# The second attention's Q, K and V projections in three fp16 passes from its third batch on

## The chip, the cores and the metric

One NeuronCore of a Trainium2 chip runs the whole program. The metric is the device time of one execution, in microseconds, lower is better. TensorE is PE in the rows, VectorE is DVE, ScalarE is ACT, GpSimd is POOL, and SyncE (SP) only issues DMAs here.

## The reference

Four layers, each an attention and then a feed-forward, work on `x` of 8 batches x 256 tokens x 128 channels, each on a layer norm of `x` with its result added to `x`. Context `ctx_1024` has the same shape. The second attention is the one that changes:

```python
q = (query @ Wq.T + bq).reshape(B, S, H, dh).transpose(0, 2, 1, 3)      # H = 16, dh = 8
k = (key @ Wk.T + bk)...;  v = (value @ Wv.T + bv)...                    # key = value = ctx
scores = jnp.einsum('bhqd,bhkd->bhqk', q, k) / SCALE + chemical_bias[:, None, :, :]
scores = jnp.where(mask == 0, -jnp.inf, scores)
attn = jax.nn.softmax(scores, axis=-1)
out = jnp.einsum('bhqk,bhkd->bhqd', attn, v)...
return out @ Wo.T + bo
```

Around it stand, in order: a wide attention (head size 64), a feed-forward over 16 experts, this attention, a feed-forward of 8 routed experts and a shared one (layer 1), a retention with a gated feed-forward (layer 2), and an attention of the same kind without mask and bias (layer 3) with a last feed-forward.

## The kernel before

The kernel writes one program for each of the five engines. Order between engines comes from semaphores alone; on one engine the instructions stand in the order in which the code issues them. `narrow_attention(layer, ...)` builds both the second attention (`layer == 1`, `masked`) and the fourth (`layer == 3`).

It goes over 8 batches with 8 units each; a unit `u` is a pair of heads, `b, n = divmod(u, 8)`. On TensorE a unit is: `weigh(u)` (L735 the shifts, L739 the transposed scores), on odd `n` `maxima` (L725, transposes of the row maxima's parts), `scores(u + 3)` (L709, and L716 adds bias and mask), `mix` (L757, probabilities by values), then, on `n` 0 to 4, `project(b + 1, n)`, a job of the next batch's projections, and on `n == 5` `out(b - 1)` (L778, L782), the output product. Jobs 0 to 3 are Q and K for half of the heads each (L684), job 4 is V (L695). Masked, each job is two fp32 matmuls, which the profile shows as four records; in the fourth attention each is made of three fp16 passes (L688, L698): weights and inputs are held as a high and a low fp16 half, and the products high x high, high x low and low x high are summed (`PASSES`).

VectorE takes in each unit the bias and mask add of the transposed scores (L937), the row maximum (L920) of the unit three ahead, on odd ones of these `cut` (L927, L929: the maxima in parts, which L725 transposes), and around it the norm of the next sublayer: `stats` (L299, L302, L305) at `n == 7`, `scale` (L330) at `n == 1`, and `norm_out` (L957, L960) and the add to `x` (L965). ScalarE does the exponentials (L857), copies the projections out of PSUM with bias and scale (L836, L841), and copies the shifts (L851).

GpSimd runs one list in order for each batch `b`: `masks_beside(b, 0)` (L911, L913), four `split_` of the projections into halves (L632, L636), `masks_beside(b, 1)`, after batch 1 `lead.weights` (the halves of the next feed-forward's weights, L2056 to L2066), then `power` of the norm two batches back (L310) and `lead.halves` (L2076, L2078). Its turn for batch `b` runs while the other engines are on the units of batch `b - 1`. In the fourth attention `weights16` (L605 to L610) halves the attention's weights, scaled by 256 in place, and `inputs16` (L620, L622) a batch's context and `xn_t`. The context tile is double-buffered and loaded by SyncE (`loads`). The retention's two loads of the context (`LOADS = 2`, L2737) are waited for by `keys` on GpSimd (L2726 on), behind the memsets of `zeros` (L2743).

## Time and profile before

| what | us |
|---|---|
| median of three runs | 1470.1 |
| lowest, highest | 1463.5, 1475.24 |
| the profiled execution: time | 1461.97 |
| its span | 1460.2 |
| second attention, about | 738 to 994 of the span |

Over the whole span TensorE is busy 90%, VectorE 71%, GpSimd 63%, ScalarE 62%; the mean granted TensorE clock is 0.956 of the full 2.4 GHz. A row of windows gives a stretch and its length, then the busy us (and instructions) of PE, PEld (weight loads), DVE, ACT and POOL, the granted TensorE clock as a share of 2.4 GHz, the DMA share and GB/s. Rows give times in us from the span's start, or durations in ns where they say so. In a line `out<-in` comes the shape (partitions x elements, type) and xcount; in brackets stands the idle time of the engine just before it and what ended it. Starts of instructions on one engine may overlap a little, as they are pipelined.

### The profile page before, as it was taken

The numbers are of one execution on the slowest core, as the hardware profiler recorded it, in microseconds if no ns is written. First come the engines' busy times: TensorE is split into PE (matmuls) and PEld (weight loads), VectorE is DVE, ScalarE is ACT, GpSimd is POOL, SyncE is SP. The second block draws the span as 40 slices with busy tenths as digits, with TensorE's granted clock in tenths as the row PEclk, the third lists the DMA queues.
The fourth block names the chain that finished last, engine by engine and source line by source line (L and its number), as shares of the span: only waits on it lengthen the run. The fifth ranks groups of instructions, "written<-read, shape, count | busy, mean of one in ns | idle before, by whom it ended". The sixth has DMA issues, their size and how long they took to land.

```text
span 1460.2 us, 37325 instructions
## 1 busy us (share of the span) xinstructions
PE 1318.7 (90%) x14582; PEld 807.8 (55%) x14582; DVE 1039.4 (71%) x2493; ACT 899.9 (62%) x1487; POOL 913.2 (63%) x879
## 2 busy tenths in 40 slices
PE   5999999997979999999979999986989799799987
PEld 3466566665757777777743433433567466344435
DVE  7888888888744344444647989986698477677775
ACT  4677787774859999999934544432234332465556
POOL 6788887876658999899857646522262120655535
PEclk9899999999989999999968999997989899799999
DMA  8000000000013110000101021000000000000000
GB/s 276 9 9 9 9 9 9 2 2 17 29 34 100 60 34 29 29 29 14 67 4 33 34 66 33 31 2 29 1 2 3 8 1 1 8 9 5 5 2 30
DMA packets 26083, 39.64 MB, mean 27 GB/s; under 512 B 7314, under 2 KB 13365, under 8 KB 25429
## 3 DMA queue, kind: packets, MB, share of 16 engines
q1 hardware_dynamic: 25364, 35.58, 7.5%
q0 software_dynamic: 576, 2.10, 0.7%
q8 instruction: 97, 1.59, 0.5%
q14 instruction: 46, 0.37, 0.1%
HBM read 38.72 MB, written 1.05 MB: 27 GB/s over the span
## 4 chain that ended last, share of the span: by engine, by line
PE 59%; DVE 25%; POOL 6%; issue 5%; ACT 4%; DMA 1%; SPq 0%; POOLq 0%; DVEq 0%; ACTq 0%
PE bank L1870 11%; PE bank L1811 10%; DVE sbuf L920 6%; PE bank L757 3%; PE bank L2336 2%; DVE sbuf L330 2%; PE bank L1264 2%; PE bank L709 2%; PE bank L1368 2%; PE bank L2094 2%; POOL sbuf L1216 2%; DVE sbuf L937 2%; PE bank L1296 2%; PE bank L1345 2%; PE bank L2315 2%
## 5 line engine op out<-in xcount | busy, mean ns | idle before, releaser
L1821 ACT ACTIVATE sbuf<-bank,sbuf 128x512 f32<-128x512 f32 (+1 forms) x512 | 323.1, 684 | 30.2 <-PE bank L1811 18.1
L1841 POOL TENSOR_TENSOR sbuf<-sbuf 128x512 f16<-128x512 f32 x256 | 304.9, 1199 | 56.4 <-ACT sbuf L1821 55.2
L1870 PEld LDWEIGHTS bank<-sbuf 128*128 128x128 f16 x3072 | 194.1, 98 | 67.4 <-issue 7.7
L1870 PE MATMUL bank<-sbuf 128*128 128x128 f16 x3072 | 214.4, 220 | 6.4 <-DVEq L1958 6.4
L310 POOL TENSOR_TENSOR sbuf<-sbuf 128x2 f32<-128x2 f32 (+1 forms) x48 | 39.7, 827 | 285.0 <-DVE sbuf L305 280.1
L1811 PE MATMUL bank<-sbuf 128*128 128x512 f16 x768 | 209.1, 382 | 0.0
L920 DVE TENSOR_REDUCE sbuf<-bank 128x4 f32<-128x1024 f32 x128 | 156.4, 1222 | 57.1 <-PE bank L709 42.2
L1953 DVE SCALAR_TENSOR_TENSOR sbuf<-bank,sbuf 128x128 f32<-128x128 f32 x256 | 71.7, 342 | 166.2 <-PE bank L1870 165.9
L1216 POOL TENSOR_TENSOR sbuf<-sbuf 128x512 f16<-128x512 f32 x128 | 147.9, 1176 | 57.1 <-ACT sbuf L1463 57.0
L757 PE MATMUL bank<-sbuf 128*32 128x256 f32 x2048 | 140.5, 394 | 1.6 <-ACT sbuf L857 1.6
L1210 POOL TENSOR_TENSOR sbuf<-sbuf 128x512 f16<-128x512 f32 x96 | 111.3, 1175 | 23.0 <-ACT sbuf L1451 22.9
L857 ACT ACTIVATE sbuf<-sbuf 128x1024 f32<-128x1024 f32 x64 | 67.6, 1057 | 90.7 <-DVE sbuf L937 90.7
L1553 DVE CUSTOM_DVE_ANT_0 bank<-bank,sbuf 128x256 f32<-128x256 f32 x256 | 100.6, 455 | 23.2 <-PE bank L1296 23.2
L632 POOL TENSOR_TENSOR sbuf<-sbuf 128x512 f16<-128x512 f32 x64 | 66.5, 1040 | 71.1 <-ACT sbuf L836 71.0
L1461 ACT ACTIVATE sbuf<-sbuf 128x1024 f32<-128x1024 f32 x64 | 68.0, 1062 | 55.0 <-DVE sbuf L1572 54.8
L937 DVE TENSOR_TENSOR sbuf<-bank,sbuf 128x1024 f32<-128x1024 f32 x64 | 78.1, 1220 | 21.9 <-PE bank L739 21.7
L757 PEld LDWEIGHTS bank<-sbuf 128*32 128x32 f32 x2048 | 54.7, 111 | 66.5 <-issue 42.2
L1572 DVE TENSOR_TENSOR sbuf<-bank,sbuf 128x1024 f32<-128x1024 f32 x64 | 78.0, 1218 | 16.1 <-PE bank L1326 15.5
L857 ACT ACTIVATE sbuf<-bank 128x1024 f32<-128x1024 f32 x64 | 65.5, 1024 | 38.5 <-PE bank L739 38.2
L836 ACT ACTIVATE sbuf<-bank,sbuf 128x256 f32<-128x256 f32 x128 | 53.4, 469 | 57.3 <-PE bank L688 29.3
L1811 PEld LDWEIGHTS bank<-sbuf 128*128 128x128 f16 x768 | 65.0, 98 | 32.1 <-issue 1.1
L1450 ACT ACTIVATE sbuf<-bank 128x512 f32<-128x512 f32 x96 | 57.4, 598 | 37.1 <-PE bank L1264 22.1
(319 smaller groups left out, 2736.9 us busy)
## 6 DMA issues: line engine op xcount, KB each, us to landing
sbuf<-w SPq DMA_DIRECT2D x32, 256.0 KB, 2.9
sbuf<-bias_t SPq DMA_DIRECT2D x4, 1024.0 KB, 12.3
sbuf<-ctx_t SPq DMA_DIRECT2D x24, 128.0 KB, 2.4
sbuf<-bias_q POOLq DMA_DIRECT2D x4, 512.0 KB, 11.4
sbuf<-mask_t SPq DMA_DIRECT2D x8, 256.0 KB, 2.7
sbuf<-bias_t SPq DMA_DIRECT2D x8, 256.0 KB, 3.0
sbuf<-mask_q SPq DMA_DIRECT2D x8, 256.0 KB, 3.6
sbuf<-bias_q SPq DMA_DIRECT2D x8, 256.0 KB, 4.2
```

The source lines that it names most:

```text
L757: last = pe.matmul(bank[O_BANK[b % 2]][32 * j:32 * j + 32, part * S:part * S + S], lhs, exps[:, (2 * Q + j // 2) % EXPS, at:at + S], start ...
L857: act.activation(exps[:, u % EXPS, :], biased[:, u % 2, :] if masked else w_pair, ACT.Exp)\
L920: v.tensor_reduce(row_max[:, (u // 2) % 2, :, at].rearrange("p m j -> p j m"), s_pair.rearrange("p (j m c) -> p j m c", j=2, c=S), AX.X, A ...
L937: v.tensor_tensor(biased[:, u % 2, :].rearrange("p (j c) -> p j c", c=HW), w_pair.rearrange("p (j c) -> p j c", c=HW), add_t[u // PER_BATC ...
L1210: g.tensor_tensor(to[1], like(x32[:, k % 2, :], to[1]), to[0], ALU.subtract).then_inc(s["halved"], 1)
L1216: g.tensor_tensor(p_low[:, u % PROBS, cols], exps[:, u % 2, cols], p_high[:, u % PROBS, cols], ALU.subtract).then_inc(s["probs"], 1)
L1553: last = v.tensor_tensor_reduce(bank[S_BANK[j]][:, cols], bank[S_BANK[j]][:, cols], add_q[u // NP % 2][:, cols], 1.0, -BIG, ALU.add, ALU.m ...
L1572: v.tensor_tensor(biased[:, u % 2, :].rearrange("p (j c) -> p j c", c=HW), w_pair.rearrange("p (j c) -> p j c", c=HW), bias_t[:, 2 * n:2 * ...
L1811: last = pe.matmul(bank[u % 4][:, :], w1_16[p][:, w, f * P:(f + 1) * P], x16[:, xk, c * CHUNK:(c + 1) * CHUNK], start=k == 0, stop=k == 2)
L1821: last = act.activation(to, bank[u % 4][:, :], ACT.Gelu, bias=b1[u // U][:, u % FT0:u % FT0 + 1], scale=1 / SCALE)
L1841: g.tensor_tensor(hid16[1][:, u % BUFS, :], hid[:, u % 4, :], hid16[0][:, u % BUFS, :], ALU.subtract)\
L1870: last = pe.matmul(bank[4 + out_no % 2][:, j * P:(j + 1) * P], hid16[h][:, u % BUFS, j * P:(j + 1) * P], w2_16[p][:, w, f * D:(f + 1) * D] ...
```

## The change

In the second attention the first two batches keep their fp32 projections. The weights are halved by GpSimd after batch 1's splits and masks, once all ten jobs of the first two batches are projected (they are scaled in place). From batch 2 on the jobs read fp16 halves, and GpSimd halves context and `xn_t` of batch `b + 1` in its turn `b`, into a single buffer (`RING16` is 1 there and stays 2 in the fourth attention), once batch `b` is fully projected. The new tiles lie in the SBUF area `body`. `lead.weights` moves from turn 1 to turn 2. The column with the scale 256 is set at the start of VectorE's program, a semaphore `sixteen` is added, and the retention loads its context with one DMA and one semaphore.

```diff
--- before.py
+++ after.py
@@ -522,7 +522,7 @@
                 "row",
                 "sixteen",
                 "hidden_keys",
-            ) if k not in (("sixteen",) if masked else ("masks", "biased", "hidden_keys"))}
+            ) if masked or k not in ("masks", "biased", "hidden_keys")}
             ctx_in = [sem(L + f"ctx_in{p}") for p in range(2)]
             mask_in = [sem(L + f"mask_in{p}") for p in range(2 * masked)]
             x0 = x_steps[0]
@@ -565,10 +565,14 @@
             shift = take([2, S], BF16)
             rden = take([S])
             att_t = take([S])
-            if not masked:
+            if masked:
+                w16 = [take([2, HG * P], F16), take([2, HG * P], F16), take([2, D], F16)]
+                x16, c16 = [take([2, S], F16)], [take([2, S], F16)]
+            else:
                 top[0] = max(top[0], 21040)
                 x16, c16 = x16 + [take([2, S], F16)], c16 + [take([2, S], F16)]
-            SCALE = 1.0 if masked else 2.0 ** 8
+            FIRST16, RING16 = 2 * masked, len(x16)
+            SCALE = 2.0 ** 8
             PASSES = ((0, 0), (0, 1), (1, 0))
             WEIGHTS = 9
             assert top[0] <= 24832
@@ -615,14 +619,14 @@
                 cols = slice(b * S, b * S + S)
                 g.wait_ge(ctx_in[b % 2], b // 2 * 16 + 16)
                 g.wait_ge(nrm_xt, nm.ready(b))
-                wait(g, s["projected"], JOBS * (b - 1))
-                for n, (to, of) in enumerate(((c16[b % 2], ctx_t[b % 2]), (x16[b % 2], xn_t[:, cols]))):
+                wait(g, s["projected"], JOBS * (b - RING16 + 1))
+                for n, (to, of) in enumerate(((c16[b % RING16], ctx_t[b % 2]), (x16[b % RING16], xn_t[:, cols]))):
                     g.tensor_copy(to[:, 0, :], of).then_inc(s["sixteen"], 1)
-                    g.wait_ge(s["sixteen"], WEIGHTS + 4 * b + 2 * n + 1)
+                    g.wait_ge(s["sixteen"], halved16(b - 1) + 2 * n + 1)
                     g.tensor_tensor(to[:, 1, :], of, to[:, 0, :], ALU.subtract).then_inc(s["sixteen"], 1)
 
             def halved16(b):
-                return WEIGHTS + 4 * b + 4
+                return WEIGHTS + 4 * (b - FIRST16) + 4
 
             def pool(g):
                 def split_(b, k):
@@ -644,9 +648,12 @@
                         split_(b, k)
                     if masked and b:
                         masks_beside(g, b, 1)
-                    if not masked and b + 1 < B:
+                    if masked and b == 1:
+                        g.wait_ge(s["projected"], FIRST16 * JOBS)
+                        weights16(g)
+                    if FIRST16 <= b + 1 < B:
                         inputs16(g, b + 1)
-                    if gated and b == 1:
+                    if gated and b == 2:
                         lead.weights(g)
                     if b >= 2:
                         after.power(g, b - 2, b - 1)
@@ -671,7 +678,7 @@
                     if k == 0:
                         pe.wait_ge(ctx_in[b % 2], b // 2 * 16 + 16)
                         pe.wait_ge(nrm_xt, nm.ready(b or late[0][0] - 1))
-                        if not masked:
+                        if b >= FIRST16:
                             pe.wait_ge(s["sixteen"], halved16(b))
                     to = job_bank(b, k)
                     xt = xn_t[:, b * S:b * S + S]
@@ -680,22 +687,22 @@
                         pair, kind = divmod(k, 2)
                         for c in range(2):
                             m = 2 * pair + c
-                            if masked:
+                            if b < FIRST16:
                                 last = pe.matmul(to[:, c * S:(c + 1) * S], (wq, wk0)[kind][:, m, :],
                                                  ct if kind else xt, start=True, stop=True)
                                 continue
                             for n, (w, half16) in enumerate(PASSES):
                                 last = pe.matmul(to[:, c * S:(c + 1) * S], w16[kind][:, w, m * P:(m + 1) * P],
-                                                 (c16 if kind else x16)[b % 2][:, half16, :],
+                                                 (c16 if kind else x16)[b % RING16][:, half16, :],
                                                  start=c == n == 0, stop=c == 1 and n == 2, skip_group_check=True)
                     else:
                         for t in range(SB):
                             o = to[:, t * P:(t + 1) * P]
-                            if masked:
+                            if b < FIRST16:
                                 last = pe.matmul(o, ct[:, t * P:(t + 1) * P], wv, start=True, stop=True)
                                 continue
                             for n, (w, half16) in enumerate(PASSES):
-                                last = pe.matmul(o, c16[b % 2][:, half16, t * P:(t + 1) * P], w16[2][:, w, :],
+                                last = pe.matmul(o, c16[b % RING16][:, half16, t * P:(t + 1) * P], w16[2][:, w, :],
                                                  start=t == n == 0, stop=t == 1 and n == 2, skip_group_check=True)
                     last.then_inc(s["projected"], 1)
 
@@ -828,13 +835,14 @@
                 def project(b, k):
                     act.wait_ge(s["projected"], b * JOBS + k + 1)
                     src = job_bank(b, k)
+                    unit = 1 / SCALE if b >= FIRST16 else 1.0
                     if k < QK:
                         wait(act, s["halved"], b * QK + k - 1)
                         pair, kind = divmod(k, 2)
                         for c in range(2):
                             bias = (bqs if kind == 0 else bk)[:, 2 * pair + c:2 * pair + c + 1]
                             last = act.activation(x32[:, k % 2, c * S:(c + 1) * S], src[:, c * S:(c + 1) * S], ACT.Identity,
-                                                  bias=bias, scale=(DH ** -0.5 if kind == 0 else 1.0) / SCALE)
+                                                  bias=bias, scale=unit * (DH ** -0.5 if kind == 0 else 1.0))
                     else:
                         wait(act, s["mixed"], 2 * GROUPS * (b - 1))
                         for t in range(SB):
@@ -842,7 +850,7 @@
                                 val[b % 2][:, t, :].rearrange("p (g c) -> p g c", g=GROUPS)[:, :, 0:HG * 32]
                                 .rearrange("p g (j c) -> p g j c", c=32)[:, :, :, 0:DH],
                                 src[:, t * D:(t + 1) * D].rearrange("p (g j d) -> p g j d", j=HG, d=DH), ACT.Copy,
-                                scale=1 / SCALE)
+                                scale=unit)
                     last.then_inc(s["evacuated"], 1)
 
                 def maxima(Q):
@@ -1499,6 +1507,7 @@
             def vector(v):
                 c = dve(v)
                 v.memset(half, -0.5)
+                v.memset(scale_col, 2.0 ** 8)
                 v.memset(ones, 1.0).then_inc(eyes_ready, 1)
                 c.step(v.memset(parts, 0.0)).settle()
                 c.step(v.memset(part_of[:, :, :, 2], -LIFT)).settle()
@@ -2693,7 +2702,7 @@
                 "gathered",
                 "back",
             )}
-            LOADS = 2
+            LOADS = 1
             c_in = [sem(f"r_c_in{k}") for k in range(LOADS)]
             x0 = x_steps[0]
             x_steps[0] += B
```

## Rows read from the trace of the kernel before

**Rows 1.** windows, layer 1: busy us (x count), clock; steady batch, last batch

```profile
880.20:908.70 28.50, 26.20 (x269) 11.30 (x265) 25.98 (x35) 13.75 (x24) 16.87 (x16) 1.00 0.14 43
965.70:994.00 28.30, 24.24 (x244) 11.47 (x237) 22.52 (x62) 8.51 (x12) 2.85 (x5) 0.87 0.00 1
```

**Rows 2.** timeline, VectorE, steady batch: start, us, instruction [idle <-releaser]

```profile
880.94 2.35 DVE L330 TENSOR_SCALAR sbuf<-sbuf 128x128 f32<-128x128 f32 x2
...
890.97 1.22 DVE L937 TENSOR_TENSOR sbuf<-bank,sbuf 128x1024 f32<-128x1024 f32 x1 [0.24 <-PE bank L739]
...
893.36 0.50 DVE L927 TENSOR_SCALAR sbuf<-sbuf 128x8 bf16<-128x8 f32 x1
...
897.95 1.22 DVE L937 TENSOR_TENSOR sbuf<-bank,sbuf 128x1024 f32<-128x1024 f32 x1 [1.39 <-PE bank L739]
...
906.53 0.32 DVE L927 TENSOR_SCALAR sbuf<-sbuf 128x8 bf16<-128x8 f32 x1
906.88 0.20 DVE L929 SCALAR_TENSOR_TENSOR sbuf<-sbuf 128x8 bf16<-128x8 f32 x1
```

**Rows 3.** waits in 794.7 to 965.7: us total, times, longest

```profile
DVE sbuf L937 <- PE bank L739: 11.8, 14, 1.4
```

**Rows 4.** single lines, whole span: count, ns min/median/max

```profile
L299 DVE BATCH_NORM_STATS2 sbuf<-sbuf x128: 272/277/296, 3.5 to 1432.4; 128x6 f32<-128x128 f32 x128
...
L305 DVE TENSOR_SCALAR sbuf<-sbuf x48: 168/170/632, 4.9 to 1433.0; 128x2 f32<-128x2 f32 x32, 128x4 f32<-128x4 f32 x16
...
L927 DVE TENSOR_SCALAR sbuf<-sbuf x64: 184/186/1115, 755.3 to 1420.4; 128x8 bf16<-128x8 f32 x64
```

**Rows 5.** timeline of VectorE, end of batch 0

```profile
784.26 1.11 DVE L927 TENSOR_SCALAR sbuf<-sbuf 128x8 bf16<-128x8 f32 x1
785.41 1.19 DVE L929 SCALAR_TENSOR_TENSOR sbuf<-sbuf 128x8 bf16<-128x8 f32 x1
```

**Rows 6.** timeline of GpSimd, layer 1

```profile
785.29 1.25 POOL L2062 TENSOR_TENSOR sbuf<-sbuf 128x640 f32<-128x640 f32 x1
...
811.17 1.27 POOL L913 TENSOR_TENSOR sbuf<-sbuf 128x512 f32<-128x512 f32 x1
...
904.28 0.72 POOL L310 TENSOR_TENSOR sbuf<-sbuf 128x2 f32<-128x2 f32 x1 [7.08 <-DVE sbuf L305]
...
906.20 1.94 POOL L911 TENSOR_SCALAR sbuf<-sbuf 128x512 f32<-128x512 int32 x1
...
932.81 0.72 POOL L310 TENSOR_TENSOR sbuf<-sbuf 128x2 f32<-128x2 f32 x1 [7.08 <-DVE sbuf L305]
```

**Rows 7.** timeline of TensorE, end of batch 0

```profile
786.65 0.39 PE L725 MATMUL bank<-sbuf 128*128 128x128 bf16 x2 [2.89 <-DVE sbuf L929]
```

**Rows 8.** windows of single stretches, columns as in rows 1

```profile
780.97:788.85 7.88, 4.38 (x38) 1.29 (x40) 6.86 (x9) 2.49 (x3) 7.47 (x9) 0.78 0.48 150
1180.29:1187.85 7.56, 6.33 (x39) 4.18 (x40) 7.43 (x10) 1.92 (x5) 7.11 (x10) 1.00 0.01 2
1312.97:1315.21 2.24, 1.74 (x24) 0.83 (x25) 1.50 (x3) 1.25 (x2) 2.08 (x5) 1.00 0.25 66
998.00:999.00 1.00, 0.82 (x8) 0.82 (x9) 0.72 (x3) 0.13 (x1) 0.73 (x2) 1.00 0.00 0
787.00:792.20 5.20, 5.20 (x35) 1.27 (x34) 2.71 (x3) 1.44 (x2) 4.93 (x4) 0.50 0.02 3
```

**Rows 9.** chain that ended last, batch 1: start us, us, engine line

```profile
793.35 1.06 PE bank L684 x4
```

**Rows 10.** the same chain in the fourth attention

```profile
1300.05 0.76 PE bank L688 x6
```

**Rows 11.** timeline of VectorE, batches 1 and 2

```profile
815.57 0.18 DVE L927 TENSOR_SCALAR sbuf<-sbuf 128x8 bf16<-128x8 f32 x1
...
824.91 1.30 DVE L330 TENSOR_SCALAR sbuf<-sbuf 128x128 f32<-128x128 f32 x2
```

**Rows 12.** timeline of GpSimd, start of the routed feed-forward

```profile
999.33 1.95 POOL L2743 MEMSET sbuf<- 128x1088 f32 x2
```

## The prediction, made before the changed kernel was run

> **What bounds the kernel now.** I read the windows by batch first, then the chain of work that ended last, then the timelines of VectorE, GpSimd and TensorE at the places that the change touches. The second attention (layer 1) repeats every 28.5 us in its steady batches. In one such stretch VectorE is busy 25.98 us and TensorE 26.20 us at full granted clock, ScalarE 13.75 and GpSimd 16.87 [rows 1]. So two engines are near their limit, and what a cheaper projection is worth depends on which of them the path runs through where the projections stand. The reader should see two things in the VectorE timeline of one batch [rows 2]: where it starts late because of TensorE, and where its own instructions are too long.
>
> First, after units with a projection VectorE is late by 0.24 us only (L937 at 890.97, waiting for L739). The longer gap, 1.39 us at 897.95, comes after the unit with the output product, which has no projection in it. Over six batches all waits of L937 for L739 sum to 11.8 us in 14 times [rows 3]; the 1.39 gap is some 6 x 1.39 = 8.3 of it, so about 3.5 us is all that faster projections could take out of these waits.
>
> Second, L330 takes 2.35 us for two instructions [rows 2]. L927 goes from 0.184 to 1.115 us and L305 from 0.168 to 0.632, while L299, whose input is in SBUF too, stays within 0.272 to 0.296 [rows 4]. Side by side the timelines show why: L929 at 785.41 ends at 786.60, and GpSimd's L2062, begun at 785.29, ends at 786.54; the L927 before it ends at 785.37, when L2062 has just taken over [rows 5, 6]. These small VectorE instructions are held until the running GpSimd instruction is over. GpSimd's own durations do not stretch. L927 and L929 lead to the maxima's transposes, and TensorE waited 2.89 us for L929 there [rows 7]; the clock then stood at 0.50 from 787.0 to 792.2 [rows 8], its lower level of 1.2 GHz.
>
> **The change part by part.** All against the profiled execution: span 1460.2, time 1461.97 us.
>
> *(a) Cheaper projections.* A Q or K job is 1.06 us for four fp32 records [rows 9] and 0.76 us for six fp16 records, which the fourth attention shows [rows 10]. That is 0.30 us a job, at most 1.5 us a batch for five jobs (the V job is smaller), 9.0 us for batches 2 to 7. The path takes little of it. In batch 1's units (jobs of batch 2) the path runs through two such jobs before VectorE takes over at 799.8, since the chain has L684 at 793.35 [rows 9] and once more, 3.7 us later: gain 0.6. In the steady batches the gain is 0.24 at L937, and then L927 at 893.36 takes 0.50 instead of 0.18 [rows 2] because GpSimd's split holds it; that split starts after ScalarE's evacuation, which itself follows VectorE's L937. An earlier L927 is held longer. I take 0.1 a batch, 0.4 in all; the ends are 0 and 3.5.
>
> *(b) Halving the weights.* The nine instructions run from 1180.29 to 1187.85 = 7.6 us in the fourth attention, and a batch's four halving instructions from 1312.97 to 1315.21 = 2.2 us [rows 8]. They come after GpSimd's masks at the end of batch 0, exactly where the next layer's weights stand now, 780.97 to 788.85 = 7.9 us [rows 8]. The same L927 and L929 meet an equally dense row of GpSimd work, and the clock drop stays. The pieces are 512 columns wide instead of 640, and L950 before them is held as well; laid side by side L929 ends about 0.3 us later: +0.3, ends -1.0 and +1.5. The new wait before them, for batch 1's projections, is met by then, and TensorE's new wait for batch 2's halves is met at about 780.97 + 7.6 + 2.2 = 790.8, while the first job of batch 2 starts at 793.35 [rows 9]: nothing, as long as the 2.5 us of distance last. If that cover were gone, TensorE would stand and L937 behind it.
>
> *(c) The next layer's weights move to batch 2's turn on GpSimd.* They now follow the masks that end at 812.44 [rows 6] and the 2.2 us of halving, so they run from about 814.7 to 822.5. Before, GpSimd was idle there for 7.08 us, as in each batch (the wait before 904.28) [rows 6]. VectorE was not: from 815.57 to 826.2 it has no gap, with L927, L929, L305, L927, L929 and L330 in it [rows 11]. So what holds them adds to the path: L927 by an L2062 (1.25 us [rows 6]) met near its start, +1.0; L929 by the shorter cast that follows, +0.7 (or 0, if it slips into the gap between two instructions); L305 by most of a subtraction as long as L2062, +1.3; the second L929 +0.6, the middle of 0 and 1.2. Queued behind the weights on GpSimd are L310, the next masks and the splits of batch 3. L310 is done at about 823.3 and L330 comes only at 824.91 plus the 3.6 us of delay: no stall. But masks and splits now run dense under L330, which takes 2.35 us as in the steady batch instead of 1.30 [rows 11]: +1.1. Sum +4.7; the ends are 0 and +6.
>
> *(d) Halving batch by batch.* 2.2 us on GpSimd after the masks of each batch, in a gap of 7.08 us [rows 6], at about 897.2 to 899.4 of the steady batch. The next instruction of the held kind, L927, comes behind L937 (897.95) and an L920 of about the same length, at 900.3 [rows 2]. So nothing; if GpSimd slipped 1 us later, L927 and L929 would lose up to 0.4 + 0.67 us each batch, 5 us in all. The single ring buffer makes it wait for the batch's own last projection, which is over before the masks are. The context tile was loaded a batch before.
>
> *(e) One load of 1 MB in the retention instead of two of 512 KB.* Both halves have landed by 998.0 (0 GB/s after it), and the first instruction that reads them stands behind two memsets that end at 1001.28 [rows 8, 12]. Cover 3.3 us, cost nothing; if that were gone, GpSimd's keys would be late, with idle time behind them. The added memset at the start and the changed scale factors in ScalarE are nothing beside this.
>
> Sum: -0.6 - 0.4 + 0.3 + 4.7 = +4.0. The profiled execution would take 1466 us. It lies 8.1 us under the median of the three runs, 1470.1; with the same distance the median becomes 1474.1.
>
> What holds VectorE is also in the Trainium skill (SBUF — State Buffer, section "Who interferes with whom"): whichever of the two issues first gets the shared pair for its whole instruction. The row of L2062 agrees. Another does not: L911 runs from 906.20 to 908.14, yet L927 of 906.53 is over in 0.32 us and L929 of 906.88 in 0.20 [rows 2, 6]. By the rule the masks moved under L927 and L929 would cost 1 to 2 us more, as an estimate; by the rows they do not.
>
> **The rivals.**
>
> *1. TensorE's relief reaches the end (chance 0.2).* For it: TensorE has more busy time than VectorE, and the chain has L684 in it. Against: the 0.24. If all 3.5 + 0.6 us came through and the hold of (c) cost half, 2.4: 0.3 + 2.4 - 4.1 = -1.4, median about 1469. The limit, with (c) at 0 and all jobs on the path, is -9, 1461.
>
> *2. The clock falls (slower; 0.12).* At 786.65 a wait of 2.89 us went with a stretch of 5.2 us at half clock; TensorE, busy throughout, then loses 2.6 us [rows 7, 8]. The last batch, with 24.24 us busy, has a mean clock of 0.87 [rows 1], and with (a) each batch falls from 26.2 to 24.7 us. One fall at batch 2's start gives +6.6, 1477. One in every steady batch gives 4.0 + 5 x 2.6 = +17, 1487; from five falls on it is over 1%. Against it: the work that goes is spread in pieces of 0.3 us, and what fell before was a wait of almost 3 us in one piece.
>
> *3. The halves are late (0.05).* If GpSimd reaches the halves of batch 2 only after 793.3, each us late is a us lost: from 2.5 us on. 2 us more than that give 1476.
>
> *4. The holds cancel (0.13).* A shift of a few tenths lets the held instructions slip through: within 1 us of before, 1470.
>
> My own case, a net +2 to +6.5, has 0.5.
>
> **How the numbers follow.** The likeliest is 1474.1. Its own range is 1472 to 1477. The runs of before spread from 1463.5 to 1475.24, so the median of the new one moves by several us without any cause; with rival 1 below and one clock fall above, 1463 to 1481. About 1%, 14.7 us, is what a measurement of this kernel can tell from no change. Only rival 2 in every batch, at 0.03, is slower by that. Faster by 1% needs the whole 9 us and more: 0.02. Within 1%: 0.95.
>
> **What would show it.** Right: in the profile after, L688 has six fp16 records for each job in the second attention from its third batch on; at about 814 to 822 GpSimd runs L2062 to L2066, and L927, L929 and L305 there are near 1 us; L330 takes about 2.3 us in all batches from 2 on; the distance between L310 of two batches stays 28.5 (904.28 to 932.81) [rows 6]. Wrong: if that distance falls by 0.3 us or more, (a) is on the path; if the clock has a new stretch of 0.50 between 815 and 960, it is rival 2; if TensorE waits for GpSimd ahead of the first fp16 job, rival 3.

## The result and the profile after

The changed kernel takes 1476.13 us (median of 20 runs, 1469.18 to 1480.67). The kernel before, measured beside it, takes 1470.2 (20 runs, 1462.63 to 1478.09). The ratio is 1.0036 with a 95% interval of 1.0018 to 1.0053: 5.3 us slower. That is inside the 1% that the prediction calls no change, but both intervals leave 1 out: a second measurement, told below, gives 1.0037 (1.0007 to 1.0066).

The profiled execution took 1475.99 us with a span of 1474.2, against 1461.97 and 1460.2 before. Those 14 us are not the change. These are two windows of the changed kernel, the tail's first stage (from the last sum of the feed-forward at 1076.11 to the gated feed-forward's first) and all behind it. Columns: window, us, then busy us (x count) of PE, PEld, DVE, ACT and POOL, granted clock, DMA share, GB/s.

```profile
1076.11:1192.34 116.23, 105.15 (x1631) 72.50 (x1632) 75.56 (x215) 37.13 (x92) 29.34 (x36) 0.80 0.02 4
1192.34:1474.20 281.86, 250.92 (x2635) 131.44 (x2633) 198.95 (x342) 143.22 (x248) 129.51 (x149) 0.96 0.03 8
```

The first of them in the second profile of the same changed kernel, and in the profile of the kernel before, in this order:

```profile
1077.21:1184.32 107.11, 98.42 (x1631) 70.61 (x1632) 75.42 (x215) 37.20 (x92) 29.32 (x36) 0.86 0.02 5
```

```profile
1075.30:1179.32 104.02, 91.95 (x1631) 66.23 (x1632) 75.31 (x215) 37.92 (x95) 29.32 (x36) 0.92 0.02 5
```

The same 1631 matmuls and 215 VectorE instructions, which the change doesn't touch, take 104, 107 and 116 us, with mean granted clocks of 0.92, 0.86 and 0.80. The changed kernel alone shows 107 and 116. So a span says nothing of 5 us here, and the readings below go by distances within the second attention. They are counted from its start, the second L310 of the stage (742.25 before, 742.47 after). The two profiles of the changed kernel give the same distance within 0.01 us at each of 13 row-maximum reduces in batches 0 and 1, and 79.15 us both to L310 of batch 2. But where the clock's stretches differ, so do the distances. `fp32_jobs` below runs the changed kernel's code up to the first job of batch 2 and is 0.4 us ahead of it there, with a first half-clock stretch of 20.5 us in place of 23.9; `fp16_in_gap` and `fp32_in_gap` share their code up to batch 4's jobs and differ by 1.15 us at L310 of batch 2. So 0.5 us of a distance, once 1.15, can be chance between executions.

Lines have moved: L927, L929, L937, L739, L911 and L913 of before are L935, L937, L945, L746, L919 and L921 after; L609, L612 and L614 halve the weights, L2065 to L2075 are `lead.weights`. VectorE and GpSimd after, end of batch 0, where [rows 5] and [rows 6] stood (start, us, instruction):

```profile
781.33 1.00 DVE L958 CAST sbuf<-sbuf 1x128 bf16<-1x128 f32 x1
782.37 0.71 DVE L960 TENSOR_TENSOR sbuf<-sbuf 1x128 bf16<-1x128 f32 x1
...
785.38 0.50 DVE L935 TENSOR_SCALAR sbuf<-sbuf 128x8 bf16<-128x8 f32 x1
785.91 0.20 DVE L937 SCALAR_TENSOR_TENSOR sbuf<-sbuf 128x8 bf16<-128x8 f32 x1
```

```profile
781.22 1.04 POOL L609 TENSOR_TENSOR sbuf<-sbuf 128x512 f32<-128x512 f32 x1
...
785.23 0.61 POOL L612 CAST sbuf<-sbuf 128x512 f16<-128x512 f32 x1
...
789.84 0.67 POOL L626 TENSOR_TENSOR sbuf<-sbuf 128x256 f16<-128x256 f32 x1
```

L958 ends at 782.33, L609 at 782.26; L935 ends at 785.88, L612 at 785.84. L937 then begins 0.01 us ahead of the next subtraction (L614 at 785.92) and goes through at 0.20 where its counterpart before took 1.19. L958 and L960, though, were held longer than their counterparts before (0.56 and 0.28 us). The halves of batch 2 are done at 790.51, as forecast (790.8).

The same two engines in batch 2's turn, where `lead.weights` now stands:

```profile
814.82 1.02 DVE L935 TENSOR_SCALAR sbuf<-sbuf 128x8 bf16<-128x8 f32 x1
815.87 0.75 DVE L937 SCALAR_TENSOR_TENSOR sbuf<-sbuf 128x8 bf16<-128x8 f32 x1
...
818.62 1.23 DVE L928 TENSOR_REDUCE sbuf<-bank 128x4 f32<-128x1024 f32 x1 [0.55 <-PE bank L723]
...
820.55 0.99 DVE L305 TENSOR_SCALAR sbuf<-sbuf 128x2 f32<-128x2 f32 x1
...
823.85 0.56 DVE L935 TENSOR_SCALAR sbuf<-sbuf 128x8 bf16<-128x8 f32 x1
...
827.43 0.90 DVE L330 TENSOR_SCALAR sbuf<-sbuf 128x128 f32<-128x128 f32 x2
```

```profile
814.54 1.25 POOL L2071 TENSOR_TENSOR sbuf<-sbuf 128x640 f32<-128x640 f32 x1
815.86 0.72 POOL L2073 CAST sbuf<-sbuf 128x640 f16<-128x640 f32 x1
...
820.12 1.39 POOL L2075 TENSOR_TENSOR sbuf<-sbuf 128x640 f16<-128x640 f32 x1
821.62 0.73 POOL L310 TENSOR_TENSOR sbuf<-sbuf 128x2 f32<-128x2 f32 x1
822.43 1.94 POOL L919 TENSOR_SCALAR sbuf<-sbuf 128x512 f32<-128x512 int32 x1
```

Three held instructions again, each over 0.03 to 0.05 us behind the GpSimd instruction that was running: 815.84 and 815.79, 816.62 and 816.58, 821.54 and 821.51. L310 has no wait at all; in steady batches it waits 4.9 us.

### The profile page after: what moved, and what is told of

It reads as the page before. It is cut to its first block, busy times and chain, and to the rows that moved or that the text cites. A ratio compares the mean times of both kernels' runs of the same rounds, so it can differ in the third digit from the quotient of the medians.

```text
span 1474.2 us, 37490 instructions
## 1 busy us (share of the span) xinstructions
PE 1325.0 (90%) x14642; PEld 810.0 (55%) x14642; DVE 1042.2 (71%) x2494; ACT 900.4 (61%) x1487; POOL 932.0 (63%) x912
## 4 chain that ended last, share of the span: by engine, by line
PE 58%; DVE 26%; POOL 6%; issue 5%; ACT 4%; DMA 1%; SPq 0%; POOLq 0%; DVEq 0%; ACTq 0%
PE bank L1879 10%; PE bank L1820 10%; DVE sbuf L928 6%; PE bank L764 3%; PE bank L2345 2%; DVE sbuf L330 2%; PE bank L1272 2%; PE bank L716 2%; DVE sbuf L945 2%; PE bank L1376 2%; POOL sbuf L1224 2%; PE bank L2324 2%; DVE sbuf L965 2%; PE bank L1304 2%; PE bank L2103 2%
## 5 line engine op out<-in xcount | busy, mean ns | idle before, releaser
L310 POOL TENSOR_TENSOR sbuf<-sbuf 128x2 f32<-128x2 f32 (+1 forms) x48 | 39.8, 829 | 277.7 <-DVE sbuf L305 272.8
L928 DVE TENSOR_REDUCE sbuf<-bank 128x4 f32<-128x1024 f32 x128 | 156.3, 1221 | 58.2 <-PE bank L716 42.6
L945 DVE TENSOR_TENSOR sbuf<-bank,sbuf 128x1024 f32<-128x1024 f32 x64 | 78.0, 1218 | 21.0 <-PE bank L746 20.9
```

Of the source, the lines that this page charges most:

```text
L928: v.tensor_reduce(row_max[:, (u // 2) % 2, :, at].rearrange("p m j -> p j m"), s_pair.rearrange("p (j m c) -> p j m c", j=2, c=S), AX.X, A ...
L945: v.tensor_tensor(biased[:, u % 2, :].rearrange("p (j c) -> p j c", c=HW), w_pair.rearrange("p (j c) -> p j c", c=HW), add_t[u // PER_BATC ...
```

## The experiments

All kernels of one group ran beside new runs of the kernel before. With 10 to 12 runs each, a ratio (not the quotient of the medians shown) resolves about 0.3%, which is 4 us. So a second measure stands beside it. Over some 115 runs of the kernel before, time and mean granted clock of the execution go together (correlation -0.91, 0.97 us less for each 0.001 of clock). The excess over that line, "at equal clock", is good to 0.5 to 1.5 us. It takes out all that goes with the mean clock, also what the kernel itself does to the clock: `delay` below has a mean clock of 0.9459 against 0.9508 over the runs of before, and of its 9.2 us in the mean only 4.3 are left. The changed kernel's two sets of runs have 0.948 and 0.949, so its 3.5 is likewise the smaller of two figures, beside 5.3. The line is one for all groups; the runs of before in the last group lie 1.0 us under it, so `fp16_in_gap` and `fp32_in_gap` are +0.6 against their own neighbours, not -0.5. The table has it last; the columns between are distances in the profile, in us after the attention's start: three row-maximum reduces on VectorE (A behind the small instructions at the end of batch 0, 788.59 in before; B in batch 1, 804.74; C behind those at the end of batch 1, 817.34), L310 of batch 2, and L310 of batch 7 against before's 219.09.

```
kernel                 A      B      C    L310 b2  L310 b7  median (runs)  ratio, 95%              at equal clock
before               46.34  62.49  75.09  77.26     0       1468.8         -                         0
changed              45.63  61.52  76.15  79.15    +2.7     1476.1 (20)    1.0036 (1.0018-1.0053)   +3.5 +-1.0
changed_again        45.64  61.52  76.15  79.15    +2.7     1473.8 (12)    1.0037 (1.0007-1.0066)   +3.5 +-1.3
fp32_jobs            45.22  61.44  75.44  78.95    +1.4     1477.1 (12)    1.0037 (1.0009-1.0066)   +3.5 +-1.1
weights_in_turn_2    43.31  59.11  73.63  75.80    -0.1     1470.8 (12)    1.0000 (0.9972-1.0027)   +0.9 +-1.3
fp16_weights_last    45.80  61.76  74.37  76.54     0.0     1472.0 (12)    1.0006 (0.9977-1.0036)   +0.6 +-1.5
weights_last         43.31  59.22  71.82  73.99    -3.2     1468.0 (12)    1.0003 (0.9975-1.0030)   -1.8 +-1.5
one_load             46.28  62.41  75.01  77.19     0.0     1474.0 (10)    1.0013 (0.9979-1.0046)   +0.3 +-1.3
delay                46.38  62.53  75.13  77.30    +6.2     1479.0 (12)    1.0066 (1.0040-1.0091)   +4.3 +-0.5
spread               43.92  59.22  71.82  73.99    -3.3     1469.1 (12)    0.9985 (0.9954-1.0017)   -1.8 +-1.0
spread_again         43.98  59.76  72.36  74.54    -2.7     1468.6 (12)    0.9981 (0.9951-1.0010)   -1.3 +-0.9
fp16_spread          45.48  61.87  74.47  76.65    +1.5     1471.6 (12)    1.0007 (0.9978-1.0036)   +1.3 +-1.4
fp16_in_gap          44.09  59.87  72.47  74.65    -1.1     1472.3 (12)    1.0012 (0.9983-1.0042)   -0.5 +-1.3
fp32_in_gap          43.68  58.73  71.33  73.50    -3.8     1468.8 (12)    1.0003 (0.9976-1.0030)   -0.5 +-1.0
```

**The next layer's weights, in three places.** `weights_in_turn_2` is before with one edit, `weights_last` is before with these weights behind the last halves, `fp16_weights_last` is the change with them there.

```diff
-                    if gated and b == 1:
+                    if gated and b == 2:
                         lead.weights(g)
```
```diff
-                    if gated and b == 1:
-                        lead.weights(g)
...
+                if gated:
+                    lead.weights(g)
                 for b in (B - 2, B - 1):
```

> The kernel before with one edit: GpSimd halves the next feed-forward's weights in turn 2 instead of turn 1. My theory, that the moved weights hold VectorE's small instructions in a stretch that had no gap: the clock fall and the 2.89 us wait at the end of batch 0 go away (gain 2.9 + 2.6 = about 5 us) and the holds at the end of batch 1 come in their place with a clock fall (cost 2 + 2.6 us), so L310 of batch 2 stands within 1 us of 819.5 and the time is that of before, +0 to +1 us. Rival, that the move alone is what the change costs: +5 us, all of it before 823. Rival, that only the fp16 work costs: -3 us or better.

> The kernel before, with the next feed-forward's weights at the very end of GpSimd's list. Nothing then holds L927 and L929 at the end of batch 0: the 2.89 us wait and the 5.2 us at half clock go, L310 of batch 2 comes 4 to 5.5 us before 819.5, and the time is 3 to 5 us under before, less up to 1 us near 978. If the clock falls there anyway, only 1 to 2 us. If what is gained is given back by the clock after the attention, the time is that of before within 1 us.

> The changed kernel, with the next feed-forward's weights halved at the very end of GpSimd's list, before the last two norms, at about 970 to 978, instead of in turn 2. If the holds at the end of batch 1 (L927 and L929 of 1.02 and 0.75 us, L305 of 0.99, a 2.22 us wait of TensorE and 6.8 us at half clock) make the loss, L310 of batch 2 comes 3 to 4 us earlier than the changed kernel's 821.6, and the time falls by 2 to 4 us, less up to 1 us of new holds near 978. If the loss of the changed kernel is made after the attention by the clock, the time does not move.

At the end `weights_last` missed its forecast of 3 to 5 us gained, and at L310 of batch 2 all three missed theirs by 0.4 to 0.7 us (3.3 for 4 to 5.5; 2.6 for 3 to 4; 1.5 ahead of before for within 1). With nothing extra on GpSimd (`weights_last`) L310 of batch 2 stands at 73.99. `lead.weights` in turn 1, as before has it, costs 3.27, all of it by reduce B (62.49 against 59.22). The halving of weights and inputs in that place costs 2.55 (`fp16_weights_last`). `lead.weights` in turn 2 costs 1.81 alone by L310 of batch 2 and, with L330 and the rest behind it, 3.16 by L310 of batch 3 (104.87 against 101.71; before has 104.98): moving this block by itself costs nothing. In the changed kernel the first block costs 2.30, and the second, together with the halving of inputs, 2.86. So 1.9 us of the change's loss is one block of GpSimd work more, at the two places where VectorE has small instructions. The costs don't simply add: 2.55 and 3.16 alone would be 5.7, and the changed kernel has 5.2 at L310 of batch 3. At the end `weights_in_turn_2` and `fp16_weights_last` can't be told from before; `weights_last` gained 3.2 us in the attention and shows -1.8 of it at equal clock. In its profile the last batch gives 3.0 back: from one L310 to the next it takes 28.0 us at a mean clock of 0.77, where before takes 25.1 at 0.93, and VectorE is busy 20.7 and 20.6 us in it. So it isn't a hold by the weights, which now run there; why the clock is lower is not shown.

**The projections alone.** `fp32_jobs` is the changed kernel with the jobs of batches 2 to 7 as fp32 matmuls on the scaled weights. All of GpSimd's work and all waits are kept.

```diff
-                            if b < FIRST16:
+                            if masked:
```

> The changed kernel, with all of GpSimd's new work and its waits, but the jobs of batches 2 to 7 are fp32 matmuls on the scaled weights. If the cheaper jobs are worth only what VectorE waits for (0.6 us in batch 1's units, nothing in the steady batches), this is 0.5 to 1.5 us slower than the changed kernel and the distance of two L310 stays 28.5 us. If TensorE's relief reaches the end it is 4 us slower or more, with a distance above 28.5. If shorter jobs cost clock, it is faster than the changed kernel: no half-clock stretch near 915, a higher mean clock, 1 to 3 us less.

It comes out as the changed kernel does, in the median and at equal clock; the forecast of 0.5 to 1.5 us slower missed. The cheaper matmuls bring nothing in the whole, though TensorE is busy 1.2 us a batch less (24.96 in a window of 28.5 us after, 26.20 in [rows 1]). Within the attention they first gain and then lose. `fp32_jobs` is 0.41 us ahead at A, before the first fp16 job, and only 0.08 at B: the fp16 jobs gain 0.3 in batch 1's units, where one step between reduces takes 3.38 us in place of 3.68. Then they lose it. L310 of batch 2, 3 and 7 is 0.2, 0.5 and 1.3 us earlier with fp32, and `fp32_jobs` has neither half-clock stretch that the changed kernel has at 816 and 915, though TensorE waits the same 2.22 us for L937 ahead of the first.

**Was the loss real?** `changed_again` is the changed kernel, unedited.

> The changed kernel once more, beside new runs of the kernel before. Theory: the change really costs something, so the median stands 3 to 6 us above that of the kernel before (1.002 to 1.004), and 2.5 to 4.5 us above it at equal mean granted clock. Rival: the 5 us of the first measurement was chance between executions; then the median is within 1.5 us of before, and so is the time at equal clock.

It is: 1.0037 again, and +3.5 at equal clock both times.

**One load.** The last part of the change alone:

```diff
-            LOADS = 2
+            LOADS = 1
```

> The kernel before with one index load of the third layer's keys in place of two, and nothing else. Forecast of the prediction: 0 us (within 1 us at equal clock), since the first keys instruction on GpSimd still comes right behind the memsets and waits for nothing. Rival: the second half of the rows comes later by the transfer, and a keys instruction shows a wait for a DMA; then up to 1 to 2 us in the third layer's gather.

(What it loads is the retention's context, not an index.) +0.3 +-1.3 at equal clock, and no distance in the attention moved by 0.1 us. Nothing that these runs resolve, as forecast.

**What a known delay is worth.**

```diff
+                    for _ in range(2 * (masked and u == 31)):
+                        c.step(v.tensor_reduce(warm[:, 0:4].rearrange("p (j m) -> p j m", m=2),
+                                               s_pair.rearrange("p (j m c) -> p j m c", j=2, c=S), AX.X, ALU.max)).settle()
```

> The kernel before with two more reduces of 1.22 us each in VectorE's queue once, in batch 3 of the second attention (what they write is not used). It measures what a known delay of about 2.4 us in one batch of the attention is worth at the end. Theory (a delay is carried on and nothing gives it back): the sum that starts each batch is 2.4 us later from batch 4 on and the whole 2.4 us slower at equal clock. Rival 1: it falls into idle time (VectorE waits 1.39 us per batch for TensorE) and is worth 1 us or less already at the next batch. Rival 2: the idle TensorE loses its clock for a stretch, and the end moves by 5 us or more.

Neither the plain theory nor the first rival; the second comes nearest. L310 of batch 4 is 6.1 us late (849.03 to 883.67 is 34.64, not 28.53), of 2.47 us put in. Here is VectorE behind the two reduces:

```profile
865.39 2.47 DVE L921 TENSOR_REDUCE sbuf<-bank 128x4 f32<-128x1024 f32 x2
...
869.38 1.13 DVE L932 SCALAR_TENSOR_TENSOR sbuf<-sbuf 128x8 bf16<-128x8 f32 x1
```

The shift moved L932 under a GpSimd instruction that it used to miss (L913, 869.20 to 870.46): 0.93 more. TensorE waited 3.39 us for L932, and from 869 on it has 10.2 us at half clock, with which the other 2.7 of the 6.1 go. By the L310 at 1049, in the routed feed-forward, 2 us are given back; +4.3 reach the end at equal clock and 9.7 by the ratio. A delay has three parts here: itself, what it is moved under, and the clock.

**The weights dealt out.** In `spread` the 8 instructions of `lead.weights` (not 14, as the expectation has it) go to turns 1 to 4 in parts of 2.0, 2.1, 2.0 and 1.4 us; each part has a place before the next small VectorE instruction.

```diff
-                    if gated and b == 1:
-                        lead.weights(g)
+                    if gated and 1 <= b <= 4:
+                        lead.weights(g, b - 1)
```

> The kernel before with the 14 GpSimd instructions of the third layer's weights, which all stood in its third turn, dealt out over turns 1 to 4 (2.0, 2.1, 2.0 and 1.4 us by the rows of before). Theory: VectorE's held instructions there go away, because each part fits into GpSimd's idle time of a turn; the sum of batch 2 comes 3 to 4 us earlier after the attention's start than before, no later turn is longer, and the whole is 3 to 4 us faster at equal clock. Rival: the tail gives it back, as in the kernel that had these weights last (2.9 us back in the last batch), and the whole is within 1.5 us of before.

> The kernel before with the third layer's weights dealt out over GpSimd's turns 1 to 4, once more, beside new runs of before. Theory: the 3.3 us that it gained in the attention are real, and about 2 us of them reach the end at equal clock. Rival: nothing reaches the end, and the first measurement of 1.9 us at equal clock was chance; then it is within 1 us of before.

One cast is held by 0.3 us and reduce A is 0.6 late, but from B on the first profile stands at the same hundredth as with no weights there at all (C at 71.82, L310 of batch 2 at 73.99). The second profile is 0.5 us later, and it is the one whose first half-clock stretch is 23.9 us as in `weights_last` (20.5 in the first). So dealt out the block costs 0 to 0.5 us in the attention, in place of 3.3. At the end the forecast of 3 to 4 us missed. Both measurements are below 1 (0.9985, 0.9981) and neither interval leaves 1 out; together, 24 runs against 58, they give 0.9986 (0.9970 to 1.0002). At equal clock -1.8 and -1.3. This is the best version found, by 1 to 2 us; two sets of a dozen runs show it at equal clock but not in the ratio.

**The change dealt out.** `fp16_spread` scales the weights in turn 1 (2.5 us), casts and subtracts in turns 2 and 3, and starts fp16 with batch 4; `lead.weights` is last.

```diff
+                    if masked and 1 <= b <= 3:
+                        weights16(g, b - 1)
...
-            FIRST16, RING16 = 2 * masked, len(x16)
+            FIRST16, RING16, SCALED = 4 * masked, len(x16), 2 * masked
```

> The changed kernel with its GpSimd work dealt out: in turn 1 only the three multiplies of the weights (2.5 us), in turn 2 the two of the q weights (1.8 us), in turn 3 those of the k and v weights (2.5 us); batches 2 and 3 keep fp32 matmuls on the scaled weights, batches 4 to 7 take three fp16 passes with context and x a batch ahead; the third layer's weights stand behind the last halves. Theory (the change's price is only where its GpSimd work stands, the cheaper matmuls are worth nothing): no turn is longer, so the reduces of batch 1 and the sum of batch 2 stand where the kernel before with these weights last has them (sum of batch 2 at 74.0 us after the attention's start, with before at 77.3 and the change at 79.2), and at equal clock it is about 2 us faster than before. Rival: the fp16 form costs something of its own in each batch, and then it stays 2 us or more behind that kernel; or it gains, and then batches 4 to 7 come in under 28.5 us each.

Missed: L310 of batch 2 at 76.65, not 74.0, and +1.3 at equal clock, not -2. The three multiplies take 2.44 us in the place where `spread` has 2.1. VectorE and GpSimd of this kernel:

```profile
783.00 1.01 DVE L973 CAST sbuf<-sbuf 1x128 bf16<-1x128 f32 x1
784.05 1.03 DVE L975 TENSOR_TENSOR sbuf<-sbuf 1x128 bf16<-1x128 f32 x1
```

```profile
782.90 2.44 POOL L608 TENSOR_TENSOR sbuf<-sbuf 128x512 f32<-128x512 f32 x3
```

Two instructions of one partition and 128 columns, 0.21 and 0.28 us in `weights_last`, take 1.0 each, 1.6 more in all. In `spread` the second of them began 0.09 us ahead of the multiply and took its 0.28. TensorE has 6.8 us at half clock at 787, where `weights_last` has 3.4. What counts more than how many us GpSimd works is which instructions of VectorE begin under it.

**The place with room.** So the multiplies and the q halves (4.3 us) went to where GpSimd waits 7.8 us in batch 0, those of k and v to turn 2; batches 4 to 7 in fp16. `fp32_in_gap` differs in the jobs alone, as `fp32_jobs` did.

```diff
+                    if masked and b == 1:
+                        g.wait_ge(s["projected"], SCALED * JOBS)
+                        weights16(g, 0)
+                        weights16(g, 1)
                     for k in range(QK):
                         split_(b, k)
```

> The changed kernel's work in other places: the three multiplies of the weights and the two of the q weights (4.3 us) behind the masks' first half that GpSimd makes for batch 1, where it then waits 7.8 us for ScalarE and VectorE has no small sbuf instruction for 4.7 us; those of the k and v weights (2.5 us) in turn 2; batches 1 to 3 in fp32 on scaled weights, 4 to 7 in three fp16 passes; the third layer's weights last. Theory (an instruction of VectorE between sbuf and sbuf is held while one of GpSimd runs, and nothing else of this work costs anything): the sum of batch 2 stands at 74.0 us after the attention's start, as in the kernel before with these weights last, against 76.7 in the kernel that dealt them over turns 1 to 3; the fp16 batches 4 to 7 lose 0.8 us once or twice where TensorE's clock falls. At equal clock 1 to 2 us faster than before. Rival: the multiplies delay batch 1's first projections or hold something else, and the sum of batch 2 stands at 76 or more.

> The kernel fp16_in_gap with the projections of batches 4 to 7 as fp32 matmuls on the scaled weights, and all work of GpSimd and all waits kept. Theory (the fall of the clock in a steady batch belongs to the fp16 matmuls, since it was seen in each profile that had them and in none without): batches 4 to 7 at 28.5 us each with no stretch at half clock, the sum of batch 7 0.8 to 1.6 us earlier than with fp16. Rival: these falls belong to GpSimd's halving of context and x, or to chance; then they stand here too.

The place works: L310 of batch 2 at 74.65 and 73.50, for 74.0 forecast. (The code is the same up to there; the 1.15 between them is a stretch of 3.4 us at half clock at 789 that only the first has, and chance.) One instruction is still held in each (L954 at 755.79 in `fp32_in_gap`, 0.97 us under the first multiply). At the end neither can be told from before, and the 1 to 2 us forecast don't show. What the pair was made for is the steady batch. L310 on GpSimd, fp16 first, then fp32:

```profile
876.36 0.72 POOL L310 TENSOR_TENSOR sbuf<-sbuf 128x2 f32<-128x2 f32 x1 [4.88 <-DVE sbuf L305]
905.62 0.72 POOL L310 TENSOR_TENSOR sbuf<-sbuf 128x2 f32<-128x2 f32 x1 [4.89 <-DVE sbuf L305]
934.15 0.72 POOL L310 TENSOR_TENSOR sbuf<-sbuf 128x2 f32<-128x2 f32 x1 [4.88 <-DVE sbuf L305]
963.44 0.73 POOL L310 TENSOR_TENSOR sbuf<-sbuf 128x2 f32<-128x2 f32 x1 [7.08 <-DVE sbuf L305]
```

```profile
900.67 0.72 POOL L310 TENSOR_TENSOR sbuf<-sbuf 128x2 f32<-128x2 f32 x1 [4.89 <-DVE sbuf L305]
929.19 0.72 POOL L310 TENSOR_TENSOR sbuf<-sbuf 128x2 f32<-128x2 f32 x1 [4.90 <-DVE sbuf L305]
957.72 0.72 POOL L310 TENSOR_TENSOR sbuf<-sbuf 128x2 f32<-128x2 f32 x1 [7.07 <-DVE sbuf L305]
```

28.52 and 28.53 us apart with fp32; with fp16 29.26, 28.53 and 29.29. Windows 8 us behind L310 of batches 4 and 6 show where, fp16 first (L310 of batch 4 stands at 872.14 with fp32):

```profile
884.50:887.50 3.00, 3.00 (x23) 0.73 (x19) 2.23 (x5) 1.33 (x2) 1.47 (x2) 0.51 0.02 5
942.50:945.50 3.00, 3.00 (x20) 0.92 (x21) 2.37 (x5) 1.33 (x2) 1.25 (x2) 0.52 0.00 0
```

```profile
880.30:883.30 3.00, 3.00 (x30) 1.37 (x28) 2.67 (x5) 1.50 (x3) 1.45 (x2) 1.00 0.00 0
937.50:940.50 3.00, 3.00 (x30) 1.38 (x28) 2.67 (x5) 1.65 (x3) 1.30 (x2) 1.00 0.02 5
```

In a stretch of 3.4 us at the lower level (1.2 GHz) TensorE gets through 23 and 20 matmuls of such a window where it does 30 otherwise, and the batch is 0.75 us longer. Of the 2.7 us between the two kernels at L310 of batch 7 these two stretches are 1.5; the forecast was 0.8 to 1.6.

Each stretch begins right behind one wait of TensorE, that for L330. Here it is in batch 4, fp16 first:

```profile
883.96 0.44 PE L339 MATMUL bank<-sbuf 128*128 128x128 f32 x2 [1.29 <-DVE sbuf L330]
```

```profile
879.73 0.44 PE L339 MATMUL bank<-sbuf 128*128 128x128 f32 x2 [0.99 <-DVE sbuf L330]
```

The 0.3 us that the cheaper job ahead of it saves is no time gained, because VectorE's L330 comes no earlier; it becomes idle time of TensorE. Over the 14 profiles this wait is 1.28 to 1.30 us 20 times, all in the fp16 kernels, and 7 of them have a fall within 1.5 us behind it. With fp32 jobs it is 0.98 to 1.00 us 37 times, and none has. Why 7 of the 20 and not the others stays open.

Each of the five profiles with fp16 jobs in this attention has one or two such stretches between 870 and 970; of the nine with fp32 jobs eight have none, and the ninth is `delay`, in the batch with the delay. In both profiles of the changed kernel the stretch is at 915 or 916, the only one in their steady batches. At the end the two kernels don't differ at equal clock (-0.5 both), so what these falls cost the whole is not shown.

## Why the prediction came out right, and where it did not

The number was right, 1474.1 against 1476.1, with the range and the sign of its own case, and so was the main mechanism, the holds where the weights moved. But the sum of +4.0 was right by errors that cancel, and in part by luck: the second measurement's median is 1473.8. By the distances, against before:

- **(a) cheaper projections: -1.0 forecast, -0.3 measured, and lost again.** In the steady batches L945 waits 11.5 us for L746 in 11 times, against 11.8 in 14 [rows 3], and L310 comes 28.5 us apart as before: not even the 0.1 a batch is there. In batch 1's units 0.3 of the 0.6 came, from A to B against `fp32_jobs`: of the two L684 on the chain [rows 9], one shortened the path by its full 0.3 and the other by next to nothing.
- **(b) halving the weights in batch 0's place: +0.3 forecast, -0.7 measured** at A (45.63 against 46.34); with (a) it is -1.0 at B. The edges of the pieces fell otherwise: L935 took 0.50 for 1.11, and L937 slipped in ahead of the next piece at 0.20 and was not held for 1.19, while L958 and L960 together took 0.87 more. Its wait on TensorE's side fell from 2.89 [rows 7] to 1.29 us, and the stretch at half clock came nevertheless (0.50 from 787.0 to 792.2 in both). The forecast's ends were -1.0 and +1.5.
- **(c) the moved weights: +4.7 forecast, +2.9 measured** from B to L310 of batch 2, and the same to L310 of batch 3 (106.91 against 104.98 after the start, and the 1.0 of B). Term by term: L927 +1.0 (measured 1.02 in place of 0.18), L929 +0.7 (0.75 for 0.20), L305 +1.3 (0.99 for 0.17, so +0.8), the second L929 +0.6 (0.19: nothing), L330 +1.1 (0.90 against 1.30, so -0.4). These make +1.8. The other 1.1 are two waits of VectorE for TensorE that before doesn't have, 0.55 ahead of L928 at 818.62 and 0.52 ahead of L945 at 825.16, and the sum had nothing for them. L330 was the most mis-sized term, and the sign "about 2.3 us in all batches from 2 on" failed in batch 2 (2.35 from batch 3 on). It met the end of one split (L640, 826.83 to 827.99), and then GpSimd waited 0.92 us for ScalarE: the splits are not dense there. The clock fell too, to 0.50 from 816.4 for 6.8 us, which the prediction had only as rival 2. Without that fall, in `fp32_jobs`, L310 of batch 2 is just 0.2 us earlier, with an L305 that isn't held (0.17) and an L330 of 2.35: what the one kernel loses to the clock the other mostly loses to L330.
- **(d), (e): nothing, and nothing measured.** Batches 3 to 7 keep 28.5 us except the one with the fall.
- **The fall in the steady batch** is rival 2 in its mild form. It cost 0.77 us once. The forecast put a fall at 2.6 us, from 5.2 us at half clock and TensorE never waiting; these are 3.4 us, and part lies in VectorE's slack. What it argued against itself was wrong, though. It held that work taken away in pieces of 0.3 us would not do it; one such piece makes the wait for L330 1.29 us long, and seven falls stand right behind such a wait.

So L310 of batch 7 is 2.7 us late: -1.0 + 2.9 + 0.8. The last batch and the feed-forward give back all but 0.6 (L310 at 1044.30, 301.83 after the start, against 301.20; the second profile has 301.85). The whole is 3.5 us late at equal clock and 5.3 in the ratio. The way from one to the other is not shown by any single profile, since one later stage alone varies by 12 us between profiles. Over the 14 rows of the table the excess at equal clock follows the shift of L310 of batch 7 (correlation 0.92, slope 0.7 us per us), but `fp32_jobs` lies 1.7 us over that line and `fp32_in_gap` is 6.2 us ahead at 1037.43 (295.03 after the start) and shows at most 0.5 of it. Why some of it comes back in the tail and some is added there stays open; that it goes through the clock is a guess, which the equal clocks don't bear out alone.

The Trainium skill's rule (SBUF — State Buffer, "Who interferes with whom") that one of the two engines holds the shared pair for a whole instruction is borne out here for every form but one, told below. The prediction's estimate that by the rule the masks that moved would cost 1 to 2 us more was not put to the test: the one that moved under L935 (823.85) was 1.42 us into its run and held it to its end, as the rule has it, and L935 took 0.56 for 0.54 before.

## What to carry to other kernels

Work on GpSimd is free only where no VectorE instruction of the kind that it holds (here L305, L330, L927, L929, L950 and L952, all from sbuf to sbuf; L299 and L302 are not held) begins under it. Lay the two timelines side by side, and deal a block of 8 us out in parts that end before the next such instruction: here that was worth 1 to 2 us at equal clock, and the cheaper matmul nothing. Where both TensorE and VectorE are near their limit, work taken from TensorE can come back as a longer wait and a fall of its clock, here 0.75 us in each batch that had one. And where executions differ by 12 us in a stage that the change doesn't touch, compare distances within the stage, take more than one profile, and give the total both as it is and at equal clock.

## What was not expected of the hardware

- Over all 14 profiles, from 740 to 1000 us, 309 of the 128x8 VectorE instructions (L927 and L929 of before) began while GpSimd was running. Under casts, multiplies, additions and subtractions all 183 ended 0.04 or 0.05 us behind the GpSimd instruction. Another 127 (97 of them at a mask instruction) began up to 0.01 us ahead of GpSimd's, and all went first, at 0.19 or 0.20.
- The exception is the mask instruction from int32, L911 or L919, 1.94 us. Under it, 126 times, one that begins 0.32 to 0.34 us in (56 times; once 0.10) is held only up to 0.65 (for 0.32 us; once 0.55), one that begins at 0.68 (57 times) is free at 0.20, and one that begins 1.41 to 1.44 in (12 times) is held to its end: L935 at 823.85 above, 0.56, under L919 of 822.43. No run has one between these places. [Rows 2, 6] show the first two kinds.
- GpSimd's own instructions hardly change: L911 takes 1.92 to 1.94 us, and 1.95 to 1.97 where a 128x8 one went just ahead of it (97 times).
- A delay of 2.47 us in VectorE's queue became 6.1 one batch later.
- Two profiles with the same wait of TensorE, 2.22 us for L937, differ in the clock behind it: 6.8 us at half clock with fp16 jobs, none with fp32 jobs (changed kernel and `fp32_jobs`).
